# A four-layer graph network on one core: attention summed by node tile instead of by window, and four passages reordered

## The reference

```python
# layer 0: SAGE, twice (relu between)
agg = segment_sum(x[src], dst) / max(in_count, 1);  y = agg @ Wl.T + b + x @ Wr.T
# layer 1: three hops
H = segment_sum(H[src] * edge_weight, dst) @ Wn[i].T + bn[i] + H @ Ws[i].T + bs[i]; elu, not after the last
# layer 2: product interaction
msg = (t1[src] + x[src] * x[dst] @ W2) / (sqrt(out_deg[src]) * sqrt(in_deg[dst])),  t1 = x @ W1
embed = where(in_count > 0, t1 + segment_sum(msg, dst), 0) + b; leaky_relu; divide by its norm
# layer 3: attention with 8 heads of 32
h = x @ W;  a_src = (h . att_src), a_dst = (h . att_dst)   per head; one more self loop per node
e = leaky_relu(a_src[src] + a_dst[dst]);  e = exp(e - segment_max(e, dst)[dst])
out = segment_sum(h[src] * e / denom[dst], dst) + bias;  layernorm with gamma, beta
```

## Time and profile before

| | us |
|---|---|
| median of 3 runs | 3459.12 |
| range of these runs | 3455.36 to 3464.09 |
| the profiled execution, its own time | 3453.95 |
| its span in the profile | 3452.1 |
| PE busy | 2828.1 (82%) |
| DVE busy | 1543.6 (45%) |
| POOL busy | 968.7 (28%) |
| ACT busy | 499.1 (14%) |

### The profile page before, as it was taken

One profiled execution on the slowest core, in us unless ns is written; L12 is line 12 of the kernel. 1 busy time (PEld: TensorE's weight loads), 2 busy tenths in 40 slices (PEclk: granted clock), 3 DMA queues, 4 the chain that ended last, 5 costly groups with the idle time before them and its releaser, 6 DMA issues. The chain is left out here.

```text
span 3452.1 us, 45405 instructions
## 1 busy us (share of the span) xinstructions
PE 2828.1 (82%) x14827; PEld 1940.1 (56%) x14828; DVE 1543.6 (45%) x4809; ACT 499.1 (14%) x1224; POOL 968.7 (28%) x887
## 2 busy tenths in 40 slices
PE   5666489688689899999999999699977996787771
PEld 2221378533378765565556555488753455777770
DVE  7999643355565400000000000600356667776778
ACT  5555300011100100010001000400120001000003
POOL 0000026777770000000000000000028724776753
PEclk9889799888899999999999999799988997888885
DMA  5444335434444244444444443032039844665651
GB/s 192 180 185 187 124 120 185 137 110 123 152 122 87 90 167 149 139 143 141 138 149 135 153 135 102 2 114 95 31 101 280 263 115 99 171 165 152 165 142 37
DMA packets 239095, 472.51 MB, mean 137 GB/s; under 512 B 101164, under 2 KB 158657, under 8 KB 238593
## 3 DMA queue, kind: packets, MB, share of 16 engines
q1 hardware_dynamic: 137441, 266.44, 24.4%
q10 hardware_dynamic: 67040, 145.77, 12.8%
q0 software_dynamic: 34368, 57.39, 6.9%
HBM read 369.66 MB, written 99.80 MB: 136 GB/s over the span
## 5 line engine op out<-in xcount | busy, mean ns | idle before, releaser
L870 PE MATMUL banks<-own_term,hidden 128*128 128x256 bf16 (+1 forms) x3750 | 631.5, 276 | 52.3 <-DVE own_term L913 33.0
L757 POOL DMA_INDIRECT table_dense_weights<-pair_weight,dst x416 | 412.5, 991 | 630.3 <-DVE in_count L958 491.0
L1222 PE MATMUL banks<-own_term,aggregate 128*128 128x391 f32 (+1 forms) x1664 | 551.9, 491 | 0.0
L870 PE MATMUL banks<-aggregate,hidden 128*128 128x256 bf16 x1875 | 517.0, 276 | 0.0
L1222 PEld LDWEIGHTS banks<-own_term,aggregate 128*128 128x128 f32 x1664 | 315.0, 189 | 232.4
L870 PEld LDWEIGHTS banks<-own_term,hidden 128*128 128x128 f16 x3750 | 371.0, 99 | 100.8 <-issue 45.3
L1261 DVE TENSOR_SCALAR x_features<-banks,hop_bias 128x391 f32<-128x391 f32 (+1 forms) x24 | 15.0, 624 | 916.5 <-PE banks L1222 916.5
L1544 POOL DMA_INDIRECT gathered_rows<-table_heads,src x144 | 174.3, 1210 | 769.4 <-DMA table_heads<-own_term 700.6
L509 PE MATMUL banks<-gathered_rows 128*128 128x400 f16 x806 | 213.4, 393 | 120.7 <-DVE gathered_rows L494 95.0
L1222 PE MATMUL banks<-aggregate 128*128 128x391 f32 (+1 forms) x832 | 277.8, 491 | 0.0
L493 DVE TENSOR_SCALAR gathered_rows<-counter_fp,aggregate 128x400 f16<-128x400 f16 x806 | 255.5, 317 | 17.8 <-PE banks L509 17.5
(11 more groups left out here) (393 smaller groups left out, 3368.0 us busy)
## 6 DMA issues: line engine op xcount, KB each, us to landing
hidden<-table_counts SPq DMA_DIRECT2D x74, 800.0 KB, 4.5
table_dense_weights<-weights_c ACTq DMA_DIRECT2D x26, 1600.0 KB, 5.6
own_term<-table_dense_weights SPq DMA_DIRECT2D x52, 782.0 KB, 4.2
own_term<-table_dense_weights SPq DMA_DIRECT2D x52, 780.5 KB, 4.2
gathered_rows<-table_edge_rows ACTq DMA_DIRECT2D x52, 512.0 KB
weights_c<-table_edge_rows ACTq DMA_DIRECT2D x52, 512.0 KB
aggregate<-table_dense_weights SPq DMA_DIRECT2D x26, 782.0 KB, 4.3
aggregate<-table_dense_weights SPq DMA_DIRECT2D x26, 780.5 KB, 4.2
```

Source lines behind the costliest of these rows:

```text
L757: e.indirect_dma_start(out=self.table, out_offset=bass.IndirectOffsetOnAxis(ap=self.place[:, t:t + 1], axis=0), in_=self.values[:, t:t + 1 ...
L870: m = e.matmul(to[:, 0:wide], lhs_of(k), piece(k, h, wide), start=(k == first and h == 0), stop=False, skip_group_check=True)
L1222: m = e.matmul(psum[b][:, 0:wide], z_block(block)[:, f * P:(f + 1) * P], streamed[tile % STREAM][:, lo:lo + wide], start=False, stop=(bloc ...
```

## The change

- The transposes of `x` and of the edge rows, with the DMA of these rows, are put behind the build, and the build no longer waits for `banks_copied`.
- The splits of `x` run tile by tile beside the transposes, and each tile's products for node tile 0 (`tail_products`) follow two tiles later. In stage 8 the same is done with `turn1` (top piece one tile ahead) and `tail_third`; the counts for Q3 are loaded when the last hop has turned.
- `load_pair_rows` loads the rows for pair step s+1 before the sums of step s. There are more steps beside Q1, and the bias add into `x` is made there in five parts.
- The MLP issues `to_hidden(c)` ahead of `from_hidden(c-1)`; mask and running sum stand behind it. The first count tile of Q2 goes to `w_a` while the MLP still runs.
- For the new attention a schedule of 440 steps (416 edge tiles and 24 changes of node tile) is made: two DMAs and about 12 DVE instructions before the hops, 10 matmuls inside hops 1 and 2, read from PSUM by DVE.
- 59 of 104 quads go through the DRAM table instead of 26.
- Attention has two parts. First all edge weights, in 26 rounds of 16 edge tiles: PE takes the scores of two node tiles from the score table in SBUF (32 matmuls of 48 columns a round, addressed by registers; no windows from DRAM), DVE makes exponents 128 columns wide, ACT the exponential. Then a merge: 440 steps, each one f32 matmul of 264 columns (one-hot by row) that adds into one of four banks of PSUM, each bank opened and closed by ACT for one node tile. 16 places of a quad each lie over the memory of `xT`, `agg` and `rows`.
- The planes are not zeroed, nothing is added to `agg` by register, and the 75 transposes and 25 adds at the end are gone.

```diff
-        banks_copied = pr.last("act")
-            e.wait_ge(*banks_copied)
...
+        def load_pair_rows(s):
+            b = s % 2
...
         def pair_steps():
+            landed = {0: load_pair_rows(0), 1: load_pair_rows(1)}
+            yield
             for s in range(STEPS):
-                pr.dma("act", s_pair_row[b], key_row[b], ...)
-                landed = pr.dma("act", s_pair_row[b], weight_row[b], ...)
-                sum_pairs(s, landed, lambda b, of: weight_row[b][:, of])
+                if 1 <= s < STEPS - 1:
+                    landed[s + 1] = load_pair_rows(s + 1)
+                sum_pairs(s, landed[s], lambda b, of: weight_row[b][:, of])
...
+        to_hidden(0)
+        for c in range(1, len(chunks)):
+            first_done = to_hidden(c)
+            from_hidden(c - 1)
+        body_done = pr.last("pe")
+        from_hidden(len(chunks) - 1)
...
+        def see_nodes(e, r, b):
+            e.load(pe_regs[0:ROUND], node_tile_at[0:1, bass.ds(r * ROUND, ROUND)])
+            e.wait_ge(s_hot_T, r + 1)
+            if not (isinstance(r, int) and r < 2):
+                e.wait_ge(s_z, r - 1)
+            for k in range(ROUND):
+                h, n = divmod(k, UNROLL)
+                at = e.snap(pe_regs[k], min_val=0, max_val=(NODE_TILES - 1) * SEEN)
+                for c in range(2):
+                    m = e.matmul(seen_bank(b, h)[:, n * SEEN:(n + 1) * SEEN], hot_T[b][c][:, k * P:(k + 1) * P],
+                                 am_flat[:, bass.ds(at + c * SEEN, SEEN)], start=(c == 0), stop=(c == 1))
+            m.then_inc(s_expanded, 1)
...
         def attention_act(e):
+            with e.Fori(0, ROUNDS // 2 - 1) as q:
+                for b in range(2):
+                    exponentiate(e, q * 2 + b)
+                    e.wait_ge(s_hot_T, q * 2 + (b + 1))
+                    load_positions(e, q * 2 + (b + 2), b)
...
+        def exponents_dve(e):
+            e.wait_ge(*max_ok)
+            e.wait_ge(*last_row)
+            expand(e, 0, 0, 0)
+            expand(e, 1, 1, 0)
+            with e.Fori(0, ROUNDS // 2 - 1) as q:
+                for b in range(2):
+                    exponents(e, q * 2 + b, b)
+                    expand(e, q * 2 + (b + 2), b, q + 1)
...
+        def merge_dve(e):
+            e.wait_ge(s_p, ROUNDS)
+            rounds, left = divmod(QUADS, PLACES)
+            scale_rows(e, 0, 0, 0)
+            for at in range(PLACES):
+                node_hots(e, at, at)
+                scale_rows(e, at + 1, (at + 1) % PLACES, (at + 1) // PLACES)
...
+        def merge_pe(e):
+            with e.Fori(0, MERGE_STEPS // (LOADS * STEPS_A_LOAD)) as i:
+                for k in range(LOADS * STEPS_A_LOAD):
+                    n = k % STEPS_A_LOAD
+                    if n == 0:
+                        e.load(pe_regs, merge_control[0:1, bass.ds(i * (LOADS * STEPS_A_LOAD) + k, STEPS_A_LOAD)])
...
+                    if k % GROUP == 0:
+                        e.wait_ge(s_hot, i * (LOADS * STEPS_A_LOAD // GROUP) + (k // GROUP + 1))
+                    e.wait_ge(s_begun, node)
+                    e.matmul(banks[:, bass.ds(bank_at, ATT_ROW)], onehot[:, k % UNROLL, :], wide_rows[:, bass.ds(row_at, ATT_ROW)],
+                             start=False, stop=False, skip_group_check=True).then_inc(s_mm, 1)
...
+        def merge_act(e):
...
+            for d in range(NODE_TILES):
+                e.wait_ge(s_mm, e.snap(ends_of_node[d], min_val=1, max_val=MERGE_STEPS + UNROLL))
+                e.copy(own[:, d, :], node_bank(d)).then_inc(s_summed, 1)
+                if d + SUM_BANKS < NODE_TILES:
+                    e.wait_ge(s_summed, d + 1)
+                    e.copy(node_bank(d + SUM_BANKS), own[:, d + SUM_BANKS, :]).then_inc(s_begun, 1)
...
+        def place_free(e, quad):
+            if quad >= PLACES:
+                e.wait_ge(s_mm, mm0 + (quad - PLACES) * GROUP + GROUP - 1 + NODE_TILES)
```

More of the change, by code:

```diff
@@ L50 @@
 TURNS = EDGE_TILES // UNROLL
-CONTROL = UNROLL + GROUPS
+ROUND = 2 * UNROLL
+ROUNDS = EDGE_TILES // ROUND
+QUADS = EDGE_TILES // GROUP
+PLACES = 16
+SUM_BANKS = 4
+STEPS_A_LOAD = 20
+LOADS = 2
+STAGED_PLACES = (0, *range(1, PLACES, 2))
+STAGED_QUADS = [q for q in range(QUADS) if q % PLACES in STAGED_PLACES]
+DIRECT_QUADS = [q for q in range(QUADS) if q % PLACES not in STAGED_PLACES]
 THIRDS = 4
@@ new lines, in place_tiles @@
+        def place_tiles(ready):
+            whole = mixed_f
+            first_tile = mixed_f.bitcast(I32)
+            t = V(lambda e: e.tensor_copy(node_tile_at[:, :], base_f), ready)
+            t = V(lambda e: e.tensor_scalar(first_tile, node_tile_at[:, :], 7, None, ALU.arith_shift_right), t)
+            V(lambda e: e.tensor_scalar(node_tile_at[:, :], first_tile, float(SEEN), None, ALU.mult), t)
+            return V(lambda e: e.scalar_tensor_tensor(out=local[:, :], in0=first_tile, scalar=-float(P), in1=dst_f,
+                                                      op0=ALU.mult, op1=ALU.add), pr.last("dve"))
@@ L896, in turn_rows @@
             m.then_inc(turned, 1)
-        for j in range(NODE_TILES):
-            x_split = split(j, x[:, j, :], top=x_top[j])
         counts_kept = (s_window_kept, KEPT_ALL)
@@ L1011, in pairs_beside, with to_hidden @@
                 next(steps, None)
-        for c, (n0, n1) in enumerate(chunks):
+        made = {}
+        def to_hidden(c):
+            n0, n1 = chunks[c]
             wdt = n1 - n0
-            made = []
             for mt in range(K_HID):
@@ L1535, in residual_gnn @@
[L1535 removed]
+        place = [wide_rows[:, k * GROUP * ATT_ROW:(k + 1) * GROUP * ATT_ROW].rearrange("p (k c) -> p k c", c=ATT_ROW)
+                 for k in range(PLACES)]
+        staging = [rows[:, 0:GROUP, :], rows[:, GROUP:UNROLL, :],
+                   flat_b[:, 0:GROUP * ATT_ROW].rearrange("p (k c) -> p k c", c=ATT_ROW), *place[0:3]]
+        DIRECT = len(staging)
+        STAGED = len(STAGED_QUADS)
+        mm0 = UNROLL
         s_staged = [pr.sem(f"staged_rows_gathered{k}") for k in range(DIRECT)]
@@ L1537, in residual_gnn @@
         s_kept_rows = [pr.sem(f"staged_rows_kept{k}") for k in range(DIRECT)]
-        s_place = [pr.sem(f"edge_rows_landed{k}") for k in range(len(places))]
-        STAGED = TURNS // RING_TURNS * GROUPS
-        def gather_group(e, turn, g, place, sem):
+        s_place = [pr.sem(f"edge_rows_landed{k}") for k in range(PLACES)]
+        kept_last = lambda d: (s_kept_rows[d], 16 * ((STAGED - d - 1) // DIRECT + 1))
+        IN_CHAIN = 3168 // (GROUP * ATT_ROW)
+        FIRST = [0, 1, 2, *range(6, PLACES), 3, 4, 5]
@@ new lines, in exponents_dve, with exponents_pe @@
+            for b in range(2):
+                exponents(e, ROUNDS - 2 + b, b)
+        def exponents_pe(e):
+            e.wait_ge(*max_ok)
+            for b in range(SUM_BANKS):
+                e.matmul(psum[b][:, 0:ATT_ROW], zeros_b[:, :], zeros_b[:, 0:1].broadcast_to([P, ATT_ROW]), start=True, stop=True)
+            see_nodes(e, 0, 0)
+            see_nodes(e, 1, 1)
+            with e.Fori(1, ROUNDS // 2) as q:
+                for b in range(2):
+                    see_nodes(e, q * 2 + b, b)
@@ new lines, in merge_act @@
+        def merge_act(e):
+            ends_of_node = [e.alloc_register(f"node_end{k}") for k in range(NODE_TILES)]
+            e.load(ends_of_node, merge_control[0:1, MERGE_STEPS:MERGE_STEPS + NODE_TILES])
+            e.wait_ge(*own_scaled)
+            e.wait_ge(s_expanded, ROUNDS)
+            for d in range(SUM_BANKS):
+                e.copy(node_bank(d), own[:, d, :]).then_inc(s_begun, 1)
+            for d in range(NODE_TILES):
[4 more added lines that the diff above has]
+                    e.copy(node_bank(d + SUM_BANKS), own[:, d + SUM_BANKS, :]).then_inc(s_begun, 1)
```

678 lines of the change are left out of this document (350 added, 328 removed).

## The result

The changed kernel takes 3320.95 us (median of 4 runs, 3318.38 to 3330.16) where the kernel before takes 3457.24 beside it: ratio 0.9609, 95% interval 0.9584 to 0.9633. Predicted were 3280 and a range of 3200 to 3360. The profiled execution is the slowest of the four, 3330.16 us with a span of 3328.3.

A forecast was written before the change was run, and what follows sets the result against it. PE was taken to bound hops and Q3, with holes in Q1, MLP and Q2; in attention PE, DVE and POOL wait for each other. Terms summed to -178.5, giving 3280 us, range 3200 to 3360.

The forecast's parts named there:

- Build first: Build's start: moving the transposes behind the build removes DVE's 7.49 us wait for PE, -7.5 us.
- splits: Splits of x before Q1: run tile by tile beside transposes and products, 32 us against 44, -12 us.
- turn1: y1 and tile 0 of Q3: top piece a tile ahead, first tile's products between, 77 us for 100.7, -23.
- Pair rows: Q1: pair rows loaded a call ahead remove DVE's waits, 216 us against 281, -65.
- MLP order: MLP: next chunk's products ahead of those needing relus cover PE's 39.3 us wait, 195 for 230, -35.
- Q2: Second pass: first count tile already in SBUF, no pair sums before its reads, 216 for 247 us, -31.
- Rival C: Transfers don't keep up: half of Q1's gain gone (+33), expansion loses 30, 3345 us; chance 0.17.
- Schedule and staging: Small instructions and products before and inside the hops, +7 us; 33 more quads gathered and written to DRAM, +5.
- Attention: New attention: exponents 235 us, 10 between, merge 240, together 485 for 490.8, -6.
- Rival B: Exponents: position loads are hidden after all, rounds of DVE's 4.45 us, 116 for 235, 3160 us; chance 0.08.
- The merge: Attention's second part: 440 PE products of 0.46 us are 203, DVE 202, POOL 208; taken as 240 (206 to 260).
- Rival A: Merge slower than 0.46 us a step: register work and clock at 1.2 GHz, 438 for 240, 3478 us; chance 0.05.

The follow-up runs named there:

- the rows late: Changed kernel with the rows of a pair step loaded right before its sums, as before the change: 3437.85 us.
- the lead alone: Kernel before the change, with only the rows of pair step s+1 asked for ahead of the sums of step s: 3348.19 us beside 3453.64.
- the wait and the rule together with the early positions: Changed kernel with positions loaded ahead of the exponential, gather places freed by a tighter rule, and one PE bank wait per four merge steps: 3234.07 us.
- the second wait: Changed kernel with PE waiting twice for the same register's value at each merge step: merge 321.6 us.
- fewer gathers: Changed kernel with 114 of 152 POOL gathers in the merge left out: merge 278.5 us.

## Why the prediction held, and where its steps did not

*Build first, splits, turn1, end:* -6.0, -14.9, -26.0, -11.5 for -7.5, -12, -23, -11. These were read off a wait with one releaser or off pace times count, and came so. No run undid them one by one; the stretches of the two traces are the evidence.

*Pair rows, MLP order, Q2:* the three terms -65, -35, -31 sum to -131, the traces to -128.1. That the MLP's 20 us too many and Q2's 17 too few nearly cancel is luck. The weak step is "the products of the next chunk ahead of those that need the relus" as what takes away the 39.3 us. It is one of two cures, and either is enough. With the rows late, the order alone leaves no wait for relus and an MLP of 203.5 us for 229.8 (with 103.5 us of DVE's work in it for 117.7). With the old order, the lead of the loads leaves 4.3 us of it in the old kernel and 3.5 in the changed one, and behind the lead the order is worth 8 us. The row named ACT as the releaser, and ACT was itself late: its queue holds the split copies, which wait for DVE's subtraction (139.1 us in the MLP, 29.9 with the lead alone), and DVE stood at the pair rows. So the lead reached into the MLP, where the forecast gave it nothing. Rival C, half the gain of Q1 lost, did not come: Q1's stretch kept 58.8 of 65. The MLP gave 20 us more than forecast because the floor of 190.68 us was busy time at a clock of 0.88; the same products (427 records) were busy for 183.2 us at 0.94 with the rows late and for 174.8 at 0.98 in the changed kernel. Q2 gave less. In Q2 the wait at its start stayed, 10.1 us for 8.0, and moving the running sum showed that the last splits hold it. The rest varies from execution to execution: with the same code up to there the first transpose behind Q2 came between 1020.7 and 1033.8 us in nine traces, the profiled one of the changed kernel the latest. From the MLP's last product to that transpose it was 228 to 238 us, so that the gain of Q2 is 14 to 24 us. The lead alone gives 6 of it, and all other parts without the lead none (252.0 us); only both together do.

*Schedule and staging:* +8.1 for +7 and +12.2 for +5. The DMA share of the expansion is 0.89 where it was 0.72, and DVE's wait for its low rows 64.0 for 50.3 us. But this stretch scatters: from its first product to its last it took 304.6 to 318.9 us in eleven traces whose edits don't touch it, 315.4 in the profiled one, and 303.2 and 304.7 in the two traces of the kernel before and of its form with the lead alone, so that the part costs 0 to 16 us. That the writes do it was not tried alone.

*Attention:* the exponents were right in mechanism and in size, 223.9 for 235, and moving the load shows that the bare flight is what bounded them (-58 us in the phase). Rival B, positions hidden, is what the kernel becomes by that edit; even then a round is 6.2 us and not DVE's 4.45, because PE's products at half clock with a register load between take 6.2. The Trainium skill ("DMA: Bandwidth & Descriptors", Rules for kernel authors) has it that a DMA is issued early and waited for late; both runs that did or undid it agree, with 62 us for the positions and 117 for the pair rows. The Trainium skill's fit for one DMA ("DMA: Bandwidth & Descriptors", Anatomy of one DMA — SWDGE (gpsimd) path) is for those that GpSimd issues, and these are ACT's; the estimate of 3.2 us from it is under all that the chain shows, the 3.4 to 4.1 us without staged rows on the way and the 4.7 to 7.7 with them.

The merge was mis-sized: 296.4 us for 240, 56 over, where the exponents were 11 under and the piece between them 3 over. Two terms of it were short. A step was taken as the product, 0.46 us; the product is 0.458, but the step 0.551, since registers, dynamic addresses and a wait on a register take the sequencer longer. And the gather was taken at 1.37 us, from the mean of the old loop, and came at 1.58. Removing parts of either gave 10 to 21 us, the wait and the rule together with the early positions 27, and 20 gathers fewer 21 more: the two chains bound different stretches of the same merge, as "three chains within 10% of each other" had it, but from a higher base. Rival A named the right suspect, the register's work at each step, with the wrong price: the clock stayed at 0.97.

Why the gather is dearer the trace shows. A gather that begins while DVE is at one of its f32 instructions of two operands in SBUF (L2125, L2131) ends 0.83 us after that instruction, or after 0.95 us, whichever is later:
```profile
2991.26 1.25 DVE L2125 TENSOR_TENSOR features_and_rows<-features_and_rows,hidden 128x1056 f32<-128x1056 f32 x1
2991.38 1.96 POOL L1710 DMA_INDIRECT features_and_rows<-table_heads,src  x1 [0.30 <-issue]
2993.64 0.96 POOL L1710 DMA_INDIRECT features_and_rows<-table_heads,src  x1 [0.30 <-issue]
```
This gives all 152 gathers of the changed kernel's merge within 0.06 us (90 held, 1.56 in the mean; 62 not, at most 0.97), and 1208 of 1234 in nine merges, that with the second wait (mean 1.09) and that with fewer gathers (1.39) among them. In the old loop 78 of 288 were held. Beside the exponents, where DVE has no such instruction of that length, POOL gathers without pause (2757 to 2850) for 1.0 us, though the DMA share is 0.77 there:
```profile
L1710 POOL DMA_INDIRECT features_and_rows<-table_heads,src x64 | 63.4, 991 | 19.5 <-issue 19.5
```
No run moved DVE's work by itself; the rule is read from the traces.

## What to carry to other kernels

Before an order is changed to cure a wait, follow the releaser back through its own queue: here one late DMA showed up under other names too (PE's waits for relus and at L698), and asking for it one step sooner was worth 105 us by itself, in a change that gains 136 in all. Two parts of a change can cure the same wait, and then their gains don't add: undo each alone before you credit one. Where a loop takes addresses or wait values from registers, price the step by the sequencer as well as by the engine, and wait once for several steps where order allows it. A stretch's busy time is no floor when its clock is below 1.

## What the runs showed of the hardware

A wait of PE against a register's value adds 0.10 us to a step when the sequencer is the bound, and nothing when the product covers it (0.458 a step with either one wait in four or a fixed row address, 0.551 with both dynamic, 0.652 with a second wait). PE's load of registers from SBUF takes 1.11 us for 16 and 1.36 for 20 (medians); at the merges' ends PE stood still around it for 1.35 to 1.82 us where the sequencer was the bound and for as little as 0.94 where the product was. POOL's gather of 128 rows is busy for 0.95 us, or until 0.83 us after the end of an f32 instruction of DVE with both operands in SBUF that was at work when it began: up to 2.04 us, and 1.09 to 1.39 in the mean of a merge. The granted clock was 0.50 through the exponents with positions early, with PE busy for 71% of the time in stretches of 4.4 us and pauses of 1.8, and 0.97 in the merge, with 84%.
